# Decoder, last layer: expert weights loaded tile by tile and used as the stationary operand

## The chip, the cores and the metric

The kernel runs on one NeuronCore of a Trainium2 chip. The metric is the time of one execution on the device in microseconds. Each engine (TensorE for matrix products, VectorE or DVE, ScalarE or ACT, GpSimd or POOL, and SyncE or SP, which only issues transfers) runs its own program in order, and semaphores tie them together. A chance is later given for "faster", "same" and "slower"; 0.2% of the time is the bound between them.

## What is computed

The kernel is a decoder of two layers over 32 sequences of 128 tokens with 128 features. Only the last step of the second layer, a mixture of experts, is touched by the change:

```python
def _L1_ffn_ref(x, gate_W, W_gate, W_up, W_down):      # 8 experts, F = 512, top 2
    xf = x.reshape(B * T, D)                           # 4096 tokens x 128
    pi = _sinkhorn(-(xf @ gate_W.T))                   # 20 iterations
    _, top_idx = jax.lax.top_k(pi, TOP_K)
    g = jnp.einsum('nd,efd->enf', xf, W_gate)
    u = jnp.einsum('nd,efd->enf', xf, W_up)
    y = jnp.einsum('enf,edf->end', jax.nn.silu(g) * u, W_down)
    out = jnp.zeros_like(xf)
    for k in range(TOP_K):
        out = out + y[top_idx[:, k], n_ar] * pi[:, k:k + 1]
    return out
x = _layernorm(x + _L1_ffn_ref(x, ...), axis=-1)
```

## The kernel before

`sinkhorn_ffn` does this step. After the routing, the 8192 pairs of token and expert are sorted by expert into NT = 71 tiles of 128 rows, each tile belonging to one expert. `ids` holds for each tile the rows of the token table `XD` in DRAM, `te` the number of its expert. The program of the 71 tiles is written out, not a loop at run time.

A tile goes through these operations. GpSimd gathers 128 rows of `XD` by an indirect transfer into one of RB = 4 buffers `XG` (`gather`, L1629). TensorE transposes it (`x_transposed`, L1864), and DVE copies the result to `xT` (`x_copy`, L1776). TensorE multiplies with `xT` as the stationary operand and 512 columns of the expert's gate and up weights as the moving one (`gate_up`, L1871 and L1872); the weights of all experts, `wg` and `wu`, 2 MB each, lie in SBUF, loaded once by SyncE at the start of the stage, and the slice is picked by a register with the expert's number. ScalarE applies Silu to the gate (`gated`, L1675), DVE multiplies with up (`product`, L1783) into `H`, which has tokens on the partitions. TensorE transposes `H` in four blocks (`h_transposed`, L1879), ScalarE copies that to `HT` (`turned`, L1681), and TensorE makes Y in four products with the blocks of `HT` as stationary operands and the rows of `wd` as moving ones (`down`, L1887). DVE copies Y out (`y_copy`, L1789), and GpSimd scatters it to the table `YD` in DRAM (`scatter`, L1634).

The order of the work is fixed by hand on each engine. TensorE's turn i holds the transposition of tile i, gate and up of tile i-1, the transposition of H of tile i-2 and down of tile i-3. DVE's turn i holds the copy of xT of tile i, the product of tile i-1 and the copy of Y of tile i-3. GpSimd issues gathers 0 to 3 and then, for each i, gather i+4 and scatter i. Scatter i waits for the copy of Y of tile i (semaphore `yc`), and gather i+4 waits until `XG` is free (semaphore `xT`). TensorE reads the expert's number in each turn (`value_load`, L1893). Before the tiles, DVE works out `te` (L1765) and, after a product of TensorE, `ids` (L1770). After the tiles, SyncE waits for the last scatter, loads Y back in 16 pieces, and DVE adds the two experts' parts (`Acc`) and applies the normalization.

Each float32 product appears in the trace as two passes, each with its own load of the stationary side (a transposition as one).

Of the kernel before, what the change touches and what calls it, by code (L numbers as in the profile page):

```python
# [1527 lines left out]
def sinkhorn_ffn(c, W, wsem, wcount, out):  # L1528
# [6 lines left out]
    RB = 4  # L1535
# [4 lines left out]
    GATE, UP, HTB, XTB, YB = (0, 1), (2, 3), (4, 5), 6, 7  # L1540
# [3 lines left out]
                     "os ot rr id te wl we xT xTc gu sg h hT hTc y yc a2 x st mv lv rs2 out")  # L1544
    gs = list(c.sems("e_", " ".join(f"g{i}" for i in range(RB))).values())
    ys = list(c.sems("e_", " ".join(f"y{i}" for i in range(RB))).values())
    yl = list(c.sems("e_", " ".join(f"l{i}" for i in range(RB))).values())
    sl = {"st": s["st"], "mv": s["mv"], "lv": s["lv"], "rs": s["rs2"]}
# [25 lines left out]
    XG = sb("XG", [P, RB, D])  # L1574
    xT = sb("xT", [D, 2, P])
    Sg = sb("Sg", [P, 2, F])
    H = sb("H", [P, 2, F])
# [3 lines left out]
    Acc = sb("Acc", [P, 2, GB, D])  # L1581
# [12 lines left out]
    with nc.Block() as block:  # L1594

        @block.sync
        def _(sp):
# [3 lines left out]
            for n in late_weights():  # L1601
                full = tuple(slice(None) for _ in W[n].shape)
                sp.dma_start(W[n][full], c.dram[f"w6_{n}"]).then_inc(s["we" if n in ("wg", "wu", "wd") else "wl"], 16)
# [20 lines left out]
        def _(pool):  # L1624

            def gather(i):
                if i >= RB:
                    pool.wait_ge(s["xT"], i - RB + 1)
                nc.gpsimd.indirect_dma_start(out=XG[:, i % RB, :], out_offset=None, in_=XD[:, :],  # L1629
                                             in_offset=bass.IndirectOffsetOnAxis(ap=ids[:, i:i + 1], axis=0)).then_inc(gs[i % RB], 16)  # L1630
# [8 lines left out]
            for i in range(RB):  # L1639
                gather(i)  # L1640
            for i in range(NT):
                if i + RB < NT:
                    gather(i + RB)
                scatter(i)
# [4 lines left out]
        def _(act):  # L1649
# [27 lines left out]
            def turned(i):  # L1677
                act.wait_ge(s["hT"], i + 1)
                if i >= 2:
                    act.wait_ge(s["y"], i - 1)  # L1680
                nc.scalar.copy(HT[:, i % 2, :], bank(HTB[i % 2])).then_inc(s["hTc"], 1)  # L1681

            for i in range(1, NT + 2):
                if i - 1 < NT:
                    gated(i - 1)
                if 0 <= i - 2 < NT:
                    turned(i - 2)

        @block.vector
        def _(dve):  # L1690
# [81 lines left out]
            def x_copy(i):  # L1772
# [3 lines left out]
                nc.vector.tensor_copy(xT[:, i % 2, :], PS[:, XTB, 0:P]).then_inc(s["xTc"], 1)  # L1776

            def product(i):
                dve.wait_ge(s["gu"], 2 * i + 2)
                dve.wait_ge(s["sg"], i + 1)  # L1780
                if i >= 2:
                    dve.wait_ge(s["hT"], i - 1)
# [302 lines left out]
```

## Time and profile before

| | us |
|---|---|
| median of 3 runs | 2434.86 (2433.98 to 2436.57) |
| profiled execution, its own time | 2434.3 |
| its span in the trace | 2432.5 |
| mean granted clock of TensorE | 0.845 of full |

| engine | busy in the span |
|---|---|
| TensorE | 1741.1 us, 72% |
| DVE | 1712.0 us, 70% |
| ScalarE | 941.0 us, 39% |
| GpSimd | 803.8 us, 33% |

The times are those of one profiled execution. Engine names in the rows: PE is TensorE's product, PEld its load of a stationary operand, which runs beside products, PEldq and SPq the sequencers, POOL is GpSimd. In the timeline "xN" is the number of merged instructions, and what stands in brackets is the idle time ahead and what ended it. "issue" is time in which nothing shown was waited for. The stage of the tiles lasts from about 2081 us of the span to 2376, the tail from there to the end.

### The profile page before, as it was taken

How to read it: one execution, taken by the hardware profiler on the slowest of the kernel's cores; microseconds unless marked ns; L12 is line 12 of the kernel's file. 1: busy time of each engine (PE TensorE's matmuls, PEld its weight loads, DVE VectorE, ACT ScalarE, POOL GpSimd, SP SyncE). 2: the span in 40 equal slices, each digit the busy share in tenths (PEclk: the TensorE clock that was granted, in tenths of full speed). 3: DMA queues.
4: the chain of work that ended last, by engine and by line, in shares of the span. 5: the costliest groups of instructions: out<-in, count | busy, mean ns of one | idle time of the engine just before them, and what ended most of it. 6: DMA issues, size and time to landing. Idle time of an engine off the chain costs nothing. (4 is left out here: it accounts for less than half of the span.)

```text
span 2432.5 us, 29879 instructions
## 1 busy us (share of the span) xinstructions
PE 1741.1 (72%) x9233; PEld 1061.5 (44%) x9233; DVE 1712.0 (70%) x3432; ACT 941.0 (39%) x1424; POOL 803.8 (33%) x773
## 2 busy tenths in 40 slices
PE   6999965655589947777877877679997221788880
PEld 3555554654556612322322332256666110455550
DVE  4999966677668828888888889869995567333326
ACT  2444431122144446456446545345553221222230
POOL 2222211222110025666566556532220000344441
PEclk9999987777789968888878888989997555899995
DMA  4000000000000000000000000000002200011113
GB/s 119 1 0 0 1 11 6 0 5 0 0 1 0 0 9 1 1 1 1 0 0 0 0 0 1 0 9 6 5 3 76 106 1 0 24 33 33 33 31 107
DMA packets 38099, 38.05 MB, mean 16 GB/s; under 512 B 7261, under 2 KB 32965, under 8 KB 37493
## 3 DMA queue, kind: packets, MB, share of 16 engines
q1 hardware_dynamic: 33461, 27.60, 3.7%
q0 software_dynamic: 4544, 9.32, 1.3%
q8 instruction: 44, 0.72, 0.1%
q14 instruction: 50, 0.41, 0.1%
HBM read 25.69 MB, written 11.21 MB: 15 GB/s over the span
## 5 line engine op out<-in xcount | busy, mean ns | idle before, releaser
L1498 PE MATMUL PS<-m_hC,identf 128*128 128x512 f32 x512 | 331.9, 735 | 146.4 <-POOL m_hC L1256 140.8
L1256 POOL TENSOR_TENSOR m_hC<-m_h,m_Cs 128x512 f32<-128x512 f32 x256 | 337.6, 1327 | 227.5 <-DVE m_h L1391 150.4
L1391 DVE TENSOR_TENSOR_SCAN m_h<-m_dA,PS 128x512 f32<-128x512 f32 x256 | 312.4, 1220 | 30.4 <-ACT m_dA L1344 19.5
L1498 PEld LDWEIGHTS PS<-m_hC,identf 128*128 128x128 f32 x512 | 102.2, 224 | 289.8 <-POOL m_hC L1256 264.2
L1386 DVE TENSOR_TENSOR PS<-PS,m_DU 128x512 f32<-128x512 f32 x256 | 178.4, 697 | 31.7 <-PE PS L1471 19.1
L1344 ACT ACTIVATE m_dA<-m_DT,m_A 128x508 f32<-128x508 f32 x256 | 178.2, 716 | 25.2 <-DVE m_h L1391 23.9
L1349 ACT COPY m_Cs<-PS 128x512 f32<-128x512 f32 x128 | 74.4, 581 | 273.6 <-PE PS L1478 273.6
L1629 POOL DMA_INDIRECT e_XG<-token_rows,e_ids x71 | 69.2, 974 | 237.0 <-DVE e_ids L1770 215.7
L82 POOL TENSOR_TENSOR ln_lv<-ln_mv,ln_eps 128x4 f32<-128x4 f32 x40 | 8.1, 202 | 361.2 <-DVE ln_mv L75 361.2
L1783 DVE TENSOR_TENSOR e_H<-PS,e_Sg 128x512 f32<-128x512 f32 x71 | 49.1, 692 | 108.9 <-PE PS L1872 99.5
L1675 ACT ACTIVATE e_Sg<-PS 128x512 f32<-128x512 f32 x71 | 42.4, 598 | 195.9 <-PE PS L1871 189.5
L1634 POOL DMA_INDIRECT expert_rows<-e_Yo,e_ids x71 | 70.2, 988 | 132.9 <-DVE e_Yo L1789 130.4
L311 ACT COPY a_PT<-PS 128x1024 f32<-128x1024 f32 x63 | 63.8, 1012 | 88.3 <-PE PS L522 88.3
L278 ACT ACTIVATE a_E<-a_DD 128x1024 f32<-128x1024 f32 x64 | 67.7, 1058 | 54.9 <-DVE a_DD L380 53.7
L311 ACT COPY k_PT<-PS 77x1024 f32<-77x1024 f32 x63 | 63.5, 1008 | 61.8 <-PE PS L522 61.8
L378 DVE TENSOR_REDUCE a_mx<-PS 128x8 f32<-128x1024 f32 x64 | 77.3, 1208 | 7.7 <-PE PS L515 7.7
L384 DVE TENSOR_REDUCE a_sm<-a_E 128x8 f32<-128x1024 f32 x64 | 77.4, 1210 | 5.8 <-ACT a_E L278 5.8
L522 PE MATMUL PS<-identf,k_E 128*77 128x128 f32 x512 | 70.5, 281 | 15.1 <-ACT k_E L278 15.1
L380 DVE TENSOR_TENSOR a_DD<-PS,a_mx 128x1024 f32<-128x1024 f32 x64 | 78.4, 1224 | 2.2
L1871 PE MATMUL PS<-e_w_wg,e_xT 128*128 x142 | 79.3, 641 | 0.0
L1148 PEld LDWEIGHTS PS<-w_ew,f_G 128*128 128x128 f32 x512 | 64.7, 191 | 32.1 <-issue 25.9
L512 PE MATMUL PS<-k_BD,k_QM 128*128 128x308 f32 x256 | 78.3, 429 | 0.0
(347 smaller groups left out, 4110.7 us busy)
## 6 DMA issues: line engine op xcount, KB each, us to landing
token_rows<-X SPq DMA_DIRECT2D x2, 2048.0 KB, 12.2
e_Y<-expert_rows SPq DMA_DIRECT2D x16, 256.0 KB, 3.7
e_w_wg<-in_w_wg SPq DMA_DIRECT2D x1, 2048.0 KB, 8.0
e_w_wu<-in_w_wu SPq DMA_DIRECT2D x1, 2048.0 KB, 12.4
e_w_wd<-in_w_wd SPq DMA_DIRECT2D x1, 2048.0 KB, 16.9
out_dram<-X SPq DMA_DIRECT2D x8, 256.0 KB, 2.3
X<-in_x SPq DMA_DIRECT2D x1, 1792.0 KB, 7.5
x_Cs<-in_ctx SPq DMA_DIRECT2D x8, 154.0 KB
```

Of the source, the lines that this page charges most:

```text
L311: nc.scalar.copy(PT[:, u % 2], PS[0:KL, 4:6, :].rearrange("p i (h q) -> p (i h) q", q=P)).then_inc(s["pt"], 1)
L378: nc.vector.tensor_reduce(m, units(hf), AX_X, ALU.max).then_inc(s["mx"], 1)
L380: nc.vector.tensor_tensor(d, units(hf), mb, ALU.subtract).then_inc(s["d"], 1)
L384: nc.vector.tensor_reduce(sm[:, u * HU:(u + 1) * HU], E[:, u % 2], AX_X, ALU.add).then_inc(s["sm"], 1)
L512: ins = nc.tensor.matmul(scores(gp), q, BD[r, par, :, b, :], start=True, stop=cross)
L1256: nc.gpsimd.tensor_tensor(hC[:, i % ND, :], hst[:, i % ND, :], Cs[:, n % ND, :], ALU.mult).then_inc(s["hC"], 1)
L1344: nc.scalar.activation(dA[:, i % ND, :, 1:P], bl(DT[:, par, ch, :])[:, :, 1:P], ACT.Exp, scale=A[:, ch, n:n + 1]).then_inc(s["dA"], 1)
L1349: nc.scalar.copy(Cs[:, n % ND, :], bank(3)).then_inc(s["Cs"], 1)
L1386: nc.vector.tensor_tensor(bank(4), bank(1 + n % 2), DU[:, par, ch, :], ALU.mult).then_inc(s["dBu"], 1)
L1391: nc.vector.tensor_tensor_scan(hst[:, i % ND, :], dA[:, i % ND].rearrange("p b l -> p (b l)"), bank(4), 0.0, ALU.mult, ALU.add).then_inc(s ...
L1498: nc.tensor.matmul(bank(5 + ch), c.identf[:, :], hC[:, i % ND, :], start=(n == 0), stop=(n == NS - 1)).then_inc(s["yacc"], 1)
L1871: nc.tensor.matmul(bank(GATE[i % 2]), xT[:, i % 2, :], one(W["wg"][:, bass.ds(e, 1), :]), start=True, stop=True).then_inc(s["gu"], 1)
```

## The change

SyncE loads each tile's gate and up weights, 512 KB, from DRAM into one of RW = 6 buffers `WT`, by an address computed from the tile's expert. It reads the number itself (`value_load`), and from the seventh tile on it waits until gate and up of the tile six before are done. The 2 MB tensors `wg` and `wu` are no longer kept. The weights lie in DRAM so that a load is 128 rows of 4 KB.

TensorE uses blocks of 128 columns of `WT` as the stationary operand and `xT` as the moving one: eight products of 128 columns a tile in place of two of 512. Their results have the hidden features on the partitions, so DVE's product writes `HT` directly; the transposition of H, ScalarE's copy of it and the buffer `H` go. TensorE's turn i then holds the transposition of tile i, gate and up of i-1 and down of i-2.

The banks of PSUM that this frees make the results of the token transposition and of down double. The ring of gathered rows has RG = 8 buffers. GpSimd issues gathers 0 to 7 first and then gather i+8 and scatter i. DVE's turn starts with the copy of Y of tile i-3. `Acc` lies over `XL`, a buffer of the routing that is no longer in use. The names of the semaphores and the call that passes arrays are changed accordingly.

```diff
-    RB = 4
+    RB, RG, RW = 4, 8, 6
...
-    GATE, UP, HTB, XTB, YB = (0, 1), (2, 3), (4, 5), 6, 7
+    GATE, UP, XTB, YB = (0, 1), (2, 3), (4, 5), (6, 7)
...
-    XG = sb("XG", [P, RB, D])
+    XG = sb("XG", [P, RG, D])
...
-    H = sb("H", [P, 2, F])
...
-    Acc = sb("Acc", [P, 2, GB, D])
+    Acc = XL[:, :, :].rearrange("p i (b d) -> p i b d", b=GB)
+    WT = sb("WT", [D, RW, 2, F])
...
-                sp.dma_start(W[n][full], c.dram[f"w6_{n}"]).then_inc(s["we" if n in ("wg", "wu", "wd") else "wl"], 16)
+                sp.dma_start(W[n][full], c.dram[f"w6_{n}"]).then_inc(s["we" if n == "wd" else "wl"], 16)
+            sp.wait_ge(s["te"], 1)
+            for i in range(NT):
+                e = nc.sync.value_load(te[0:1, i:i + 1], min_val=0, max_val=NE - 1)
+                if i >= RW:
+                    sp.wait_ge(s["gu"], 2 * (i - RW) + 2)
+                sp.dma_start(WT[:, i % RW, :, :], c.dram["w6_wgu"][bass.ds(e, 1), :, :, :].rearrange("o d w f -> d (o w) f")).then_inc(wt[i % RW], 16)
...
             def gather(i):
-                if i >= RB:
-                    pool.wait_ge(s["xT"], i - RB + 1)
-                nc.gpsimd.indirect_dma_start(out=XG[:, i % RB, :], out_offset=None, in_=XD[:, :],
-                                             in_offset=bass.IndirectOffsetOnAxis(ap=ids[:, i:i + 1], axis=0)).then_inc(gs[i % RB], 16)
+                if i >= RG:
+                    pool.wait_ge(s["xT"], i - RG + 1)
+                nc.gpsimd.indirect_dma_start(out=XG[:, i % RG, :], out_offset=None, in_=XD[:, :],
+                                             in_offset=bass.IndirectOffsetOnAxis(ap=ids[:, i:i + 1], axis=0)).then_inc(gs[i % RG], 16)
...
-            for i in range(RB):
+            for i in range(RG):
                 gather(i)
             for i in range(NT):
-                if i + RB < NT:
-                    gather(i + RB)
+                if i + RG < NT:
+                    gather(i + RG)
                 scatter(i)
...
-            def turned(i):
-                act.wait_ge(s["hT"], i + 1)
-                if i >= 2:
-                    act.wait_ge(s["y"], i - 1)
-                nc.scalar.copy(HT[:, i % 2, :], bank(HTB[i % 2])).then_inc(s["hTc"], 1)
-
-            for i in range(1, NT + 2):
-                if i - 1 < NT:
-                    gated(i - 1)
-                if 0 <= i - 2 < NT:
-                    turned(i - 2)
+            for i in range(NT):
+                gated(i)
...
-                nc.vector.tensor_copy(xT[:, i % 2, :], PS[:, XTB, 0:P]).then_inc(s["xTc"], 1)
+                nc.vector.tensor_copy(xT[:, i % 2, :], PS[:, XTB[i % 2], 0:P]).then_inc(s["xTc"], 1)
...
-                    dve.wait_ge(s["hT"], i - 1)
-                nc.vector.tensor_tensor(H[:, i % 2, :], bank(UP[i % 2]), Sg[:, i % 2, :], ALU.mult).then_inc(s["h"], 1)
+                    dve.wait_ge(s["y"], i - 1)
+                nc.vector.tensor_tensor(HT[:, i % 2, :], bank(UP[i % 2]), Sg[:, i % 2, :], ALU.mult).then_inc(s["h"], 1)
...
             for i in range(NT + 3):
+                if 0 <= i - 3 < NT:
+                    y_copy(i - 3)
                 if i < NT:
                     x_copy(i)
                 if 0 <= i - 1 < NT:
                     product(i - 1)
-                if 0 <= i - 3 < NT:
-                    y_copy(i - 3)
...
-            pe.wait_ge(s["we"], 48)
+            pe.wait_ge(s["we"], 16)
 
             def x_transposed(i):
-                pe.wait_ge(gs[i % RB], landed(i))
-                if i:
-                    pe.wait_ge(s["xTc"], i)
-                nc.tensor.transpose(PS[:, XTB, 0:P], XG[:, i % RB, :], c.identf[:, :]).then_inc(s["xT"], 1)
-
-            def gate_up(i, e):
+                pe.wait_ge(gs[i % RG], 16 * (i // RG + 1))
+                if i >= 2:
+                    pe.wait_ge(s["xTc"], i - 1)
+                nc.tensor.transpose(PS[:, XTB[i % 2], 0:P], XG[:, i % RG, :], c.identf[:, :]).then_inc(s["xT"], 1)
+
+            def gate_up(i):
                 pe.wait_ge(s["xTc"], i + 1)
+                pe.wait_ge(wt[i % RW], 16 * (i // RW + 1))
                 if i >= 2:
                     pe.wait_ge(s["h"], i - 1)
-                one = lambda ap: ap.rearrange("p o f -> p (o f)")
-                nc.tensor.matmul(bank(GATE[i % 2]), xT[:, i % 2, :], one(W["wg"][:, bass.ds(e, 1), :]), start=True, stop=True).then_inc(s["gu"], 1)
-                nc.tensor.matmul(bank(UP[i % 2]), xT[:, i % 2, :], one(W["wu"][:, bass.ds(e, 1), :]), start=True, stop=True).then_inc(s["gu"], 1)
-
-            def h_transposed(i):
+                for w, banks in enumerate((GATE, UP)):
+                    for f in range(FC):
+                        ins = nc.tensor.matmul(PS[:, banks[i % 2], f * P:(f + 1) * P], WT[:, i % RW, w, f * P:(f + 1) * P], xT[:, i % 2, :], start=True, stop=True)
+                    ins.then_inc(s["gu"], 1)
+
+            def down(i, e):
                 pe.wait_ge(s["h"], i + 1)
                 if i >= 2:
-                    pe.wait_ge(s["hTc"], i - 1)
+                    pe.wait_ge(s["yc"], i - 1)
                 for f in range(FC):
-                    ins = nc.tensor.transpose(PS[:, HTB[i % 2], f * P:(f + 1) * P], H[:, i % 2, f * P:(f + 1) * P], c.identf[:, :])
-                ins.then_inc(s["hT"], 1)
-
-            def down(i, e):
-                pe.wait_ge(s["hTc"], i + 1)
-                if i:
-                    pe.wait_ge(s["yc"], i)
-                for f in range(FC):
-                    ins = nc.tensor.matmul(PS[:, YB, 0:D], HT[:, i % 2, f * P:(f + 1) * P], W["wd"][:, bass.ds(e * FC + f, 1), :].rearrange("p o d -> p (o d)"), start=(f == 0), stop=(f == FC - 1))
+                    ins = nc.tensor.matmul(PS[:, YB[i % 2], 0:D], HT[:, i % 2, f * P:(f + 1) * P], W["wd"][:, bass.ds(e * FC + f, 1), :].rearrange("p o d -> p (o d)"), start=(f == 0), stop=(f == FC - 1))
                 ins.then_inc(s["y"], 1)
 
             expert = {}
-            for i in range(NT + 3):
+            for i in range(NT + 2):
                 if i < NT:
                     expert[i] = nc.tensor.value_load(te[0:1, i:i + 1], min_val=0, max_val=NE - 1)
                     x_transposed(i)
                 if 0 <= i - 1 < NT:
-                    gate_up(i - 1, expert[i - 1])
+                    gate_up(i - 1)
                 if 0 <= i - 2 < NT:
-                    h_transposed(i - 2)
-                if 0 <= i - 3 < NT:
-                    down(i - 3, expert.pop(i - 3))
+                    down(i - 2, expert.pop(i - 2))
...
-            "wg": ([D, 8, 512], F32), "wu": ([D, 8, 512], F32), "wd": ([P, 32, D], F32)}
+            "wd": ([P, 32, D], F32)}
...
-    w["w6_wg"], w["w6_wu"] = (a["L1_ffn_W_" + n].transpose(2, 0, 1) for n in ("gate", "up"))
+    w["w6_wgu"] = np.stack([a["L1_ffn_W_" + n].transpose(0, 2, 1) for n in ("gate", "up")], 2)
```

## Rows read from the trace of the kernel before

**Rows 1.** Busy time by stretch, with clock, DMA share, GB/s: start, middle of the tiles
```profile
2084.00:2092.00 8.00, 6.80 (x11) 3.02 (x12) 1.47 (x4) 1.20 (x2) 2.84 (x3) 0.57 0.13 33
2125.00:2250.00 125.00, 105.92 (x526) 68.81 (x524) 38.63 (x93) 36.70 (x62) 60.45 (x62) 1.00 0.12 34
```

**Rows 2.** Groups by line, 2081 to 2376: busy, mean ns, idle before and releaser
```profile
L1864 PE MATMUL PS<-identf,e_XG 128*128 128x128 f32 x71 | 22.4, 315 | 48.0 <-DMA e_XG<-token_rows,e_ids 48.0
```

**Rows 3.** Chain of waits over two tiles: start us, us, what
```profile
2168.62 0.33 PE PS L1864
2168.95 1.00 PE PS L1871 x2
2169.95 0.86 PE PS L1872 x2
2170.81 0.44 PE PS L1879 x4
2171.24 0.91 PE PS L1887 x8
...
2172.18 0.30 DVE e_Yo L1789
...
2172.74 0.99 POOL expert_rows L1634
...
2174.04 2.69 DMA e_XG<-token_rows,e_ids
```

**Rows 4.** Timeline of TensorE, one turn without a hole: start us, us
```profile
2092.58 0.27 PE L1864 MATMUL PS<-identf,e_XG 128*128 128x128 f32 x1
2092.69 1.02 PE L1871 MATMUL PS<-e_w_wg,e_xT 128*128 x2
2093.55 1.02 PE L1872 MATMUL PS<-e_w_wu,e_xT 128*128 x2
2094.41 0.60 PE L1879 MATMUL PS<-identf,e_H 128*128 128x128 f32 x4
2094.85 1.06 PE L1887 MATMUL PS<-e_w_wd,e_HT 128*128 x8
2095.74 0.27 PE L1864 MATMUL PS<-identf,e_XG 128*128 128x128 f32 x1
```

**Rows 5.** Third stage, line L1148: durations min/median/max ns, and eight passes in the timeline
```profile
L1148 PEld LDWEIGHTS PS<-w_ew,f_G x512: 186/192/192, 692.9 to 854.3; 128*128 128x128 f32 x171
...
702.56 1.05 PE L1148 MATMUL PS<-w_ew,f_G 128*128 128x128 f32 x8
```

**Rows 6.** GpSimd's gathers: durations min/median/max ns, and the first one
```profile
L1629 POOL DMA_INDIRECT e_XG<-token_rows,e_ids x71: 943/972/1209, 2081.4 to 2360.8; - x71
...
2081.43 1.21 POOL L1629 DMA_INDIRECT e_XG<-token_rows,e_ids  x1 [215.69 <-DVE e_ids L1770]
```

**Rows 7.** Reads and transfers: durations ns; last two: KB each, us to landing
```profile
L1893 PEldq TENSOR_LOAD <-e_te x71: 296/301/483, 2080.6 to 2361.3; - x71
L1765 DVE CAST e_te<-e_tef x1: 197/197/197, 2074.3 to 2074.3; 128x71 int32<-128x71 f32 x1
L216 SPq DMA_DIRECT2D k_Cs<-in_ctx x7: 296/297/315, 1589.8 to 1771.0; - x7
...
e_w_wg<-in_w_wg SPq DMA_DIRECT2D x1, 2048.0 KB, 8.0
...
e_w_wd<-in_w_wd SPq DMA_DIRECT2D x1, 2048.0 KB, 16.9
```

**Rows 8.** Busy time by stretch as in rows 1: stage start, tail start
```profile
1870.00:1885.00 15.00, 15.00 (x75) 15.00 (x74) 1.15 (x6) 3.54 (x7) 0.00 (x0) 0.50 1.00 280
2376.00:2380.00 4.00, 0.00 (x0) 0.00 (x0) 0.00 (x0) 0.00 (x0) 0.00 (x0) 0.50 0.62 182
```

**Rows 9.** Timeline: the last token transposition and the last scatter
```profile
2363.51 0.27 PE L1864 MATMUL PS<-identf,e_XG 128*128 128x128 f32 x1
...
2374.00 0.97 POOL L1634 DMA_INDIRECT expert_rows<-e_Yo,e_ids  x1 [0.77 <-DVE e_Yo L1789]
```

More of the change, by code:

```diff
@@ L1543, in sinkhorn_ffn @@
     s = c.sems("e_", "xd xTp xL lg la rm rd re rs rl ra cm cT gm dg gM cd ce cs ct cl ca t w mb rk v tt "
-                     "os ot rr id te wl we xT xTc gu sg h hT hTc y yc a2 x st mv lv rs2 out")
-    gs = list(c.sems("e_", " ".join(f"g{i}" for i in range(RB))).values())
+                     "os ot rr id te wl we xT xTc gu sg h y yc a2 x st mv lv rs2 out")
+    gs = list(c.sems("e_", " ".join(f"g{i}" for i in range(RG))).values())
     ys = list(c.sems("e_", " ".join(f"y{i}" for i in range(RB))).values())
     yl = list(c.sems("e_", " ".join(f"l{i}" for i in range(RB))).values())
+    wt = list(c.sems("e_", " ".join(f"w{i}" for i in range(RW))).values())
     sl = {"st": s["st"], "mv": s["mv"], "lv": s["lv"], "rs": s["rs2"]}
@@ L1788, in y_copy @@
                     dve.wait_ge(ys[i % RB], landed(i - RB))
-                nc.vector.tensor_copy(Yo[:, i % RB, :], PS[:, YB, 0:D]).then_inc(s["yc"], 1)
+                nc.vector.tensor_copy(Yo[:, i % RB, :], PS[:, YB[i % 2], 0:D]).then_inc(s["yc"], 1)
             for i in range(NT + 3):
+                if 0 <= i - 3 < NT:
+                    y_copy(i - 3)
                 if i < NT:
@@ L2073 @@
     lay = layout(a)
-    need = ["x", "ctx", "identf", "identb"] + [f"w{ph}_{n}" for ph, ws in plan_weights().items() for n in ws] + ["w4_cwr"] + [f"w6_{n}" for n in late_weights()]
+    need = ["x", "ctx", "identf", "identb"] + [f"w{ph}_{n}" for ph, ws in plan_weights().items() for n in ws] + ["w4_cwr"] + [f"w6_{n}" for n in late_weights()] + ["w6_wgu"]
     nc = _bacc.Bacc("TRN2", target_bir_lowering=False, num_devices=1)
```

## Prediction, made before the changed kernel was run

> **What bounds the kernel now.** I read the page first, then the busy time by stretch, then the chain of waits inside one stretch, then the timeline of the same instructions. The reader should see four things in that order. The expert stage, where the change lies, keeps TensorE busy 85% of a middle stretch at a granted clock of 1.00, the upper level of 2.4 GHz, with DMA at 0.12 [rows 1]. So TensorE is not quite the limit. The grouped view names what it waits for: 48.0 us idle ahead of the token transposition L1864, all until the gather of e_XG has landed [rows 2]. The chain of waits over two tiles gives the loop: TensorE 0.33 + 1.00 + 0.86 + 0.44 + 0.91 us, the copy of Y 0.30, the scatter's issue on GpSimd 0.99, then the next gather, 2.69 from issue to landing, and three hand-overs (about 0.6): 2168.62 to 2176.73, 8.1 us for two tiles [rows 3]. The cause is in the code: GpSimd queues gather i+5 behind scatter i, and scatter i waits for Y of tile i, which TensorE makes in turn i+3. Transposition i+5 stands only two turns later, so of each pair one turn (3.2) hides nothing. From transposition 3 (2092.58) to transposition 70 (2363.51) are 67 tiles in 270.93 us, 4.04 each [rows 4, 9].
>
> **The floor of TensorE before.** Early on the gathers are ahead and a turn has no hole: transpositions at 2092.58 and 2095.74, 3.16 us [rows 4]. Its parts by starts: token transposition 0.11, gate 0.86, up 0.86, H transposition 0.44, down 0.89. The gate starts at 2092.69 and up at 2093.55, so 512 columns in two passes take 0.86. The eight passes of down, 128 columns each and each with its own stationary load, start 2094.85 and give way at 2095.74: 0.111 each. The third stage's passes with weights as the stationary side show the same, eight in 1.05 of which the last lasts 0.275: 0.78 / 7 = 0.111 [rows 5].
>
> **The change part by part.**
>
> Gate and up: out go 4 passes of 512 columns (1.72), in come 8 products of 128 columns, two passes each: 16 x 0.111 = 1.78. Plus 0.06 us a tile. The form is that of the down product and of rows 5. Bounds for a pass: 0.107 (what a pass of 512 columns costs per 128, 0.43 / 4) and 0.112. I take 0.111, since the rows are of the very form.
>
> Transposition of H and ScalarE's copy of it: minus 0.44 on TensorE. The copy is off TensorE's path in full stream and gives nothing there; it gives its time once, at the drain. DVE's product writes the same bytes to HT.
>
> New turn: 0.11 + 1.78 + 0.89 = 2.78 us, if nothing is late.
>
> Gather ring of eight: gather i+9 is now queued behind scatter i, and Y of tile i is made in turn i+2, so six turns (16.7 us) lie ahead of its use. It needs 0.3 (copy) + 0.3 + 0.99 + 0.3 + 2.7 = 4.6. The wait of rows 2 goes. What is late next is GpSimd itself: a gather 0.972 [rows 6], a scatter 0.99 and behind each a gap of 0.30 (the scatter ends at 2173.73, the gather starts at 2174.04 [rows 3]), 2.56 a tile, 0.22 under TensorE. The eight gathers at the start, from 2081.43 on [rows 6], end near 2091.8, before scatter 0 can be wanted, at about 2093.6.
>
> Weights by SyncE: 71 loads of 512 KB (128 rows of 4 KB), 37 MB, where 4 MB came once before. SyncE's work for one: reading the expert's number, priced by TensorE's own, 0.30, then a transfer at a computed address, also 0.30, as k_Cs has it [rows 7]; with as much again for registers, range checks and the wait it is 1.2 us of 2.78, an estimate, and it would have to double to matter. Nothing is queued behind it on SyncE but the tail's loads, and the last weights are issued about five turns before the end. The ring's wait is for gate_up i-6, so about five turns, 14 us, are left for the landing. Cost of one transfer: the loads of wg and wd, two apart, landed 8.9 us apart although issued within 1 us, so 2 MB take 4.45 and 512 KB 1.1 us of all engines; from below, at the 280 GB/s of the 512-byte rows of token_rows, 1.9 us [rows 7, 8]. With the gathers and scatters, 0.12 of 4.04 = 0.5, DMA is busy 1.6 to 2.4 us of 2.78. It holds, and 14 us cover a landing of 3 to 5. That cover gone (a turn's weights one turn late) costs a whole 2.78 once, not per tile. The first six start at 2074.5, when the expert numbers are cast [rows 7], and the first is wanted once the first gather, issued at 2081.43, has landed (after 2084) and is transposed. They overlap the first gather: 0 to 0.5 us, I take 0.
>
> The Trainium skill, DMA: Bandwidth & Descriptors, "Anatomy of one DMA", fits 2.0 us plus bytes by 436 GB/s: 3.2 us for one such load. Were loads made one at a time, the sum would be 30 us higher; the trace overlaps the fixed part of queued loads, as the 8.9 us above show.
>
> DVE a tile: two copies of 0.29 and the product 0.69, 1.27 of work; the product can start 0.2 after the up product (2.09 into the turn) and ends at 2.78, and down of that tile is wanted 1.9 into the next turn. The earlier place of y_copy, the doubled banks XTB and YB, Acc laid over XL, and ScalarE with Silu alone each have at least 1 us of room: nothing. The two reads of 4 MB taken from the stage's start run beside the routing, on which nobody waits: nothing.
>
> **The sum.** Turns 0 to 2 run mostly at the lower level of the clock (0.57 granted, against 1.00 right behind it [rows 1]); they stream as many columns after as before, so I leave their time. Only turn 2 ends with down (0.89) where it had H's transposition (0.44): transposition 3 is at 2093.03. Transposition 70 is at 2093.03 + 67 x 2.785 = 2279.6. From there two turns less a token transposition (5.5 to the start of the last down, which the last product releases), 1.05, the copy 0.33, and a scatter that has to wait for the one before it (0.5 in all): 7.5 us, where it was 10.5 from 2363.51 to 2374.00 [rows 9]. The last scatter is at 2287.1, 86.9 us earlier; the tail is the same. The profiled execution took 2434.3 (span 2432.5): 2347.4. The median of the three runs lies 0.6 higher, 2434.86: **2348 us**. Of the gain, 67 x 0.88 = 59 us are the wait for gathers and 67 x 0.375 = 25 are TensorE's work.
>
> **Rivals.**
>
> GpSimd becomes the bound. The traffic of DMA grows fivefold beside it. The one price above the median is the first gather's 1.209 [rows 6]. If both operations cost that, a tile is 2 x 1.51 = 3.02: plus 17 us, 2365. It decides from 1.09 an operation on. For it: 92% load, no slack for jitter. Against: a spread of 943 to 1209 with all but few at 972. Chance 0.15.
>
> The weights' transfers pace the tiles. At the 182 GB/s of the stretch in which the tail's loads start [rows 8], the 655 kB of a tile (524 of weights, 65.5 each gathered and scattered) take 3.6 us: plus 58, 2406. One at a time at 3.2, the page's fit above, 2377. Against: those stretches are short of queued work, and a ring of six is not. Chance 0.09, half for each.
>
> Stationary loads no longer hide. Before, four of a turn's 17 passes load weights ahead of 512 columns; afterwards all 25 have 128 columns. A load shows 0.192 busy [rows 5]. If passes went at that, a turn is 24 x 0.192 + 0.11 = 4.72, 0.68 above 4.04: plus 46, 2481, slower than before. It decides at (4.04 - 0.11) / 24 = 0.164 a pass. Against: runs of eight at 0.111, in two stages; longer runs no row shows. Chance 0.03. The Trainium skill, TensorE: Matmul & The Clock Gate, "The mechanism" in Part 3, says that a stationary load overlaps a running matmul only where the row groups differ, which is this rival's rule; the rows of down disagree with it. Other ways to be slower (a stall of instruction supply, a late ring throughout): 0.02.
>
> The change does not loosen the loop: the scatter's landing, for which y_copy waits four tiles later, or an order I misread keeps 4.04. Then within a few us of before, 2432. Chance 0.03.
>
> **How the numbers follow.** Forecast 0.68 (2339 to 2356: the lower end is 0.107 a pass, 24 x 0.004 x 71 = 7 us, with a little of the start; the upper 0.1 us a turn of jitter), GpSimd 0.15, transfers 0.09, no loosening 0.03, slower 0.05. The range 2339 to 2385 holds the forecast, GpSimd and the page's serial case, some 0.87 nominally, and 8 in 10 once I allow for causes not named. A measurement tells about 0.2%, 5 us, from no change. Faster 0.92, same 0.03, slower 0.05.
>
> **What would show it.** Right: token transpositions 2.78 us apart; the token transposition's idle until the gather near nothing; passes with the weights WT at 0.111; GpSimd idle 0.2 a tile until e_Yo; DMA share 0.5 to 0.8 in the stage; the first weights landed before the first transposed tokens are there; the last scatter at 2287. Wrong: a TensorE wait on WT (transfers), GpSimd idle near zero with longer operations (GpSimd), passes further apart (loads), or a granted clock under 1.00 after the start.

## The result, and the profile after

| | before | after |
|---|---|---|
| median of the runs, us | 2434.76 (2433.98 to 2436.57) | 2376.64 (2376.30 to 2377.49) |
| ratio | | 0.9761, 95% interval 0.9744 to 0.9778 |
| span of the profiled execution, us | 2432.5 | 2374.5 |
| mean granted clock | 0.844 | 0.842 |

The kernel is 58.1 us faster. The forecast was 2348, a gain of 87, so 29 us of it did not come, although the time lies in the range. The runs below say which part came, and the trace says where the other part is lost; what causes the loss they leave open.

The busy time by stretch of the changed kernel: us, then busy (x instructions) of PE, PEld, DVE, ACT and POOL, clock, DMA share, GB/s. The first row answers to the middle stretch of [rows 1]; the last is taken where the gathers and the loads of weights are over.

```profile
2100.00:2200.00 100.00, 92.37 (x793) 88.82 (x792) 35.95 (x94) 19.11 (x32) 61.05 (x63) 1.00 0.67 206
2302.00:2310.00 8.00, 8.00 (x75) 8.00 (x73) 3.54 (x9) 1.67 (x3) 2.85 (x3) 1.00 0.09 27
```

TensorE has holes again, 7.6 us in 100; DMA went from 0.12 to 0.67, inside the forecast 0.5 to 0.8, and the clock is at its upper level in both stretches. The groups by line from 2070 to 2325 answer to [rows 2]:

```profile
L1871 PE MATMUL PS<-e_xT,e_WT 128*128 128x128 f32 x1136 | 144.9, 281 | 11.2 <-DVE e_xT L1774 9.8 <-issue 1.3
L1641 POOL DMA_INDIRECT expert_rows<-e_Yo,e_ids x71 | 70.1, 988 | 75.2 <-DVE e_Yo L1787 64.4 <-issue 10.8
L1636 POOL DMA_INDIRECT e_XG<-token_rows,e_ids x71 | 69.0, 972 | 237.1 <-DVE e_ids L1768 215.7 <-issue 19.8 <-PE PS L1862 1.5
```

The 48.0 us until a gather are gone. What TensorE waits for instead is VectorE's copy of the transposed tokens, L1774. GpSimd's operations last what they did, 0.97 and 0.99, and GpSimd is idle 64.4 us, 0.9 a tile, until Y is copied: it does not set the pace, it is kept waiting. The waits of TensorE, its side of loads (PEld) above all, and of SyncE's queue from 2095 to 2300 (us in total, times, longest) say the same. The only other result that TensorE waits for is DVE's product, four times, and no wait for weights is among them:

```profile
PEld PS L1871 <- DVE e_xT L1774: 14.5, 20, 0.8
PEld PS L1879 <- issue: 5.5, 5, 2.0
PE PS L1879 <- DVE e_HT L1781: 4.5, 4, 1.8
SPq L1610 <- PE PS L1871: 125.4, 56, 5.8
```

Why is the copy late, with 0.28 us of work in a turn of 2.79? The timeline of one turn and the next, 2203.8 to 2208.4 (start, us, engine, line; in brackets the idle time before):

```profile
2203.87 1.06 PE L1879 MATMUL PS<-e_w_wd,e_HT 128*128 x8
...
2204.76 0.27 PE L1862 MATMUL PS<-identf,e_XG 128*128 128x128 f32 x1
...
2204.87 1.95 PE L1871 MATMUL PS<-e_xT,e_WT 128*128 128x128 f32 x16
2205.87 0.97 POOL L1636 DMA_INDIRECT e_XG<-token_rows,e_ids  x1 [0.30 <-issue]
...
2207.55 0.27 PE L1862 MATMUL PS<-identf,e_XG 128*128 128x128 f32 x1
2207.79 0.29 DVE L1787 COPY e_Yo<-PS 128x128 f32<-128x128 f32 x1 [2.99 <-PE PS L1879]
2207.91 0.60 ACT L1682 ACTIVATE e_Sg<-PS 128x512 f32<-128x512 f32 x1 [4.14 <-PE PS L1871]
2208.00 0.28 DVE L1774 COPY e_xT<-PS 128x128 f32<-128x128 f32 x1
2208.33 0.97 PEld L1871 LDWEIGHTS PS<-e_xT,e_WT 128*128 128x128 f32 x8 [0.75 <-DVE e_xT L1774]
```

Where two rows of a timeline have "..." between them, rows are left out. Down ends at 2203.87 + 1.06 = 2204.93, the token transposition at 2205.03, and the gate, the first eight of the sixteen passes, at 2204.87 + 7 x 0.111 + 0.28 = 2205.93. VectorE and ScalarE stand idle and wait for these three results, yet take them up at 2207.79 and 2207.91: 2.9 us late for Y, 2.0 for Silu, and the copy of xT, third in line, 3.0. Two engines that don't wait for each other wake together, so what is late is TensorE's signal and not a consumer. From this TensorE loses 0.75. I call this "late signals". In the turns of tiles 67 to 70, behind the last gather (its issue starts at 2295.53), each result is taken up within 0.04 to 0.14 us of its pass, and turns are 2.79.

The trace also records when each semaphore was raised, and that shows it directly. The increment that belongs to the down of 2204.93 stands at 2207.77, the transposition's at 2207.80, those of gate and up at 2207.89 and 2207.99, and those of the next down and transposition at 2208.08 and 2208.11: six in 0.34 us. The scatter's landing, for which a copy of Y waits too, is not what is late: all 28 copies of Y that came over 0.3 us late to an idle VectorE start within 0.06 us of an increment for Y. (Where the increment stands over 1.5 us behind its pass, the view names no pass and says "remote".)

One regularity shows when the signals come. Between 2095 and 2295 there are 28 bursts of four or more increments less than 0.15 us apart. At the start of each GpSimd is idle, and its last operation was a gather, which ended 0.87 to 1.24 us before. The seven other kernels with late signals below show the same (169 bursts, 0.74 to 1.54 us). That ties the release in time to GpSimd's gathers. It does not show that they are the cause: GpSimd also comes to stand idle because the copy of Y is late, and other runs below have the same gathers and no late signal.

Over tiles 8 to 60 a copy of xT starts 2.16 us after the end of its transposition on average, and up to 4.3. A late start of up to about 2.2 us costs TensorE nothing, since the gate product is that much later in its queue; what goes beyond that is a hole, mostly in every second turn: 2.79, then 3.57. Three turns are longer still (5.27, 5.94 and 5.45, 8.3 us over 2.79 together); there down also waits 1.0 to 1.8 us for DVE's product. A fourth, of 4.51, has another reason. Behind the hole of 2270 to 2275 the granted clock went to its lower level for 3.4 us, and the sixteen passes of gate and up took 3.64 us instead of 1.95:

```profile
2270.00:2275.00 5.00, 2.98 (x26) 2.70 (x24) 1.68 (x4) 1.19 (x2) 2.27 (x3) 1.00 0.22 60
2275.00:2280.00 5.00, 4.95 (x30) 4.79 (x29) 1.27 (x3) 0.60 (x1) 3.33 (x4) 0.66 0.70 235
```

### The profile page after: what moved, and what is told of

Its sections match the earlier page's. It is cut to its first block and busy times, and to the rows that moved or that the text cites. A ratio compares the mean times of both kernels' runs of the same rounds, so it can differ in the third digit from the quotient of the medians.

```text
span 2374.5 us, 31088 instructions
## 1 busy us (share of the span) xinstructions
PE 1706.1 (72%) x9801; PEld 1104.6 (47%) x9801; DVE 1704.7 (72%) x3432; ACT 899.1 (38%) x1353; POOL 803.6 (34%) x773
## 5 line engine op out<-in xcount | busy, mean ns | idle before, releaser
L1871 PE MATMUL PS<-e_xT,e_WT 128*128 128x128 f32 x1136 | 144.9, 281 | 11.2 <-DVE e_xT L1774 9.8
L1871 PEld LDWEIGHTS PS<-e_xT,e_WT 128*128 128x128 f32 x1136 | 135.7, 195 | 16.8 <-DVE e_xT L1774 14.5
L1781 DVE TENSOR_TENSOR e_HT<-PS,e_Sg 128x512 f32<-128x512 f32 x71 | 49.0, 691 | 73.2 <-PE PS L1871 55.0
L1641 POOL DMA_INDIRECT expert_rows<-e_Yo,e_ids x71 | 70.1, 988 | 75.2 <-DVE e_Yo L1787 64.4
L1148 PEld LDWEIGHTS PS<-w_ew,f_G 128*128 128x128 f32 x512 | 64.7, 191 | 32.1 <-issue 25.8
```

The costliest lines, as they stand in the source:

```text
L1871: ins = nc.tensor.matmul(PS[:, banks[i % 2], f * P:(f + 1) * P], WT[:, i % RW, w, f * P:(f + 1) * P], xT[:, i % 2, :], start=True, stop=True)
```

## Experiments

Twelve kernels ran in three batches, each batch on a chip of its own; I call them chip A (the first four), B (the next four) and C (the last four). That turned out to matter. In the fences of code "..." stands for lines of the edit that are not shown. The kernel before measured 2435.22, 2436.41 and 2434.78 on them; on which chip the two executions shown above ran is not known.

**a_ring8: the gather ring alone (A).** The kernel before with eight buffers for gathered tokens and Acc laid over XL, products in the old form.

```
-    RB = 4
+    RB, RG = 4, 8
...
-    XG = sb("XG", [P, RB, D])
+    XG = sb("XG", [P, RG, D])
...
-                if i >= RB:
-                    pool.wait_ge(s["xT"], i - RB + 1)
+                if i >= RG:
+                    pool.wait_ge(s["xT"], i - RG + 1)
...
```

> The kernel before with one part of the change alone: the ring of gathered rows has eight buffers instead of four (Acc laid over XL to make room); wg and wu stay resident, H is still transposed. Theory: the gather's wait is gone and a turn is the 3.16 us of TensorE's own work, 67 x 0.88 = 59 us less than before, about 2376 us, which is the time of the changed kernel. Rival: something else in the loop holds the old kernel at 4.04 us a turn, 2435 us; or it lies in between if TensorE's signals arrive late here too.

Measured: 2376.43, ratio 0.9759 (0.9743 to 0.9775). The stretch 2100 to 2200, columns as above:

```profile
2100.00:2200.00 100.00, 100.00 (x537) 67.84 (x536) 37.36 (x96) 37.25 (x63) 61.72 (x64) 1.00 0.15 43
```

Turns are 3.16, with no hole. The ring alone brings as much as the whole change: 0.9759 against 0.9761. Signals are on time here but for a few: three of the 52 copies of xT of tiles 8 to 59 start over 0.3 us late. Those of tiles 59, 61, 63 and 65 start 0.96 to 1.30 us late (the first of them is one of the three), so the old form is not free of late signals on this chip. So the 25 us for TensorE's shorter turn are what is missing.

**b_noload: no loads of weights behind the first six (A).** SyncE stops after the first six tiles; the others multiply by those, so the stream of 512 KB loads is gone.

```
-            for i in range(NT):
+            for i in range(RW):
                 e = nc.sync.value_load(te[0:1, i:i + 1], min_val=0, max_val=NE - 1)
...
-                pe.wait_ge(wt[i % RW], 16 * (i // RW + 1))
+                pe.wait_ge(wt[i % RW], 16)
```

> The changed kernel in which SyncE loads only the first six tiles' weights; all later tiles use what lies in the ring (so most tiles are multiplied with the wrong expert's weights, TensorE's work is the same). Theory: what holds back TensorE's signals in the changed kernel comes with SyncE's stream of loads (its waits, reads, issues or bytes), so turns are 2.79 us as in the last six tiles, about 2350 us. Rival: the hold-up comes from TensorE's dense stream of stationary loads itself, or from GpSimd's transfers; then it stays at 3.2 us a turn, 2376 us.

Measured: 2388.49, ratio 0.9807 (0.9791 to 0.9824); DMA share 0.14, and it is slower, not faster. (Its first gather starts at 2085.36 of the span, the changed kernel's at 2081.11, so some 4 us of the 12 more stand ahead of the tiles.)

```profile
2100.00:2200.00 100.00, 88.09 (x735) 84.28 (x734) 34.77 (x88) 16.46 (x29) 57.65 (x59) 1.00 0.14 39
```

Signals are late by up to 4.4 us, and 12 of 100 us are holes. SyncE's stream of transfers is not needed for them.

**c_small: the same loads with 64 KB from the seventh tile on (A).** The rest of a buffer keeps the weights of earlier tiles.

```
+                n = F if i < RW else 64
...
-                sp.dma_start(WT[:, i % RW, :, :], c.dram["w6_wgu"][bass.ds(e, 1), :, :, :].rearrange("o d w f -> d (o w) f")).then_inc(wt[i % RW], 16)
+                sp.dma_start(WT[:, i % RW, :, 0:n], c.dram["w6_wgu"][bass.ds(e, 1), :, :, 0:n].rearrange("o d w f -> d (o w) f")).then_inc(wt[i % RW], 16)
```

> The changed kernel with the same 71 loads, reads and waits of SyncE, but from the seventh tile on only 64 of 512 columns of gate and up are loaded (64 KB instead of 512 KB; the rest of the weights is left from earlier tiles). If the bytes and their DMA traffic hold up the signals: about 2350 us, 2.8 us a turn. If SyncE's waits, reads or issues do: unchanged, 2376 us.

Measured: 2378.98, ratio 0.9773 (0.9756 to 0.9789), signals late. The bytes are not needed for it either.

**e_waith: SyncE waits for VectorE's h, not for TensorE's gu (A).**

```
-                    sp.wait_ge(s["gu"], 2 * (i - RW) + 2)
+                    sp.wait_ge(s["h"], i - RW + 1)
```

> The changed kernel in which SyncE's wait for a free buffer is on DVE's product of the tile six before (semaphore h) and not on TensorE's own semaphore gu; everything else is the same. If TensorE's signals are late because SyncE waits on one of them: about 2350 us. If bytes, reads or issues are the cause: 2376 us within 0.3%.

Measured: 2379.23, ratio 0.9768 (0.9752 to 0.9784), signals late. That SyncE listens to TensorE is not the cause.

**g_nogather: gathers for the first eight tiles alone (B).** Later tiles multiply the rows that lie in the ring.

```
             for i in range(NT):
-                if i + RG < NT:
-                    gather(i + RG)
                 scatter(i)
...
-                pe.wait_ge(gs[i % RG], 16 * (i // RG + 1))
+                pe.wait_ge(gs[i % RG], 16)
```

> The changed kernel in which GpSimd gathers only the first eight tiles (later tiles multiply the rows that lie in the ring, so most of the result is of the wrong tokens); one operation of GpSimd a tile, the scatter, is left. Theory A: TensorE's signals are held while GpSimd issues its indirect transfers back to back, which it does at 2.57 us of 2.79 a tile. Then with half of them turns are 2.79 us: about 2350 us. Theory B: TensorE's own dense stream of stationary loads holds its signals, whatever GpSimd does: 3.2 us a turn or more, 2376 to 2390 us.

Measured: 2353.53, ratio 0.9662 (0.9646 to 0.9678), turns of 2.79, signals on time. Taken alone this says that the gathers hold the signals. The next three say that it can't be taken alone.

**h_up256: a_ring8 with half an up product from the third tile on (B).** The other half is left out. A turn of the old form as short as the new one.

```
-                nc.tensor.matmul(bank(UP[i % 2]), xT[:, i % 2, :], one(W["wu"][:, bass.ds(e, 1), :]), ...)
+                n = F if i < 2 else F // 2
+                nc.tensor.matmul(PS[:, UP[i % 2], 0:n], xT[:, i % 2, :], one(W["wu"][:, bass.ds(e, 1), 0:n]), ...)
```

> The kernel before with the ring of eight, and from the third tile on the up product has 256 columns instead of 512 (half of up is left from earlier tiles, so the result is wrong): a turn of TensorE is 3.16 - 0.43 = 2.73 us, with the old form of products (weights as the moving side). Theory A (GpSimd's back-to-back transfers set the pace at which signals are late): late signals and turns well above 2.73, 3.0 or more, so 2365 us or more. Theory B (the new form's 25 stationary loads a turn): signals on time, 2.73 us, about 2376 - 29 = 2347 us.

Measured: 2346.83, ratio 0.9634 (0.9617 to 0.9650), turns of 2.73, signals on time with all the gathers at full pace.

**v_ahead: one more turn for the copy of xT (B).** xT gets four buffers, and each turn multiplies gate and up for the tile before last, so a late copy would be covered.

```
-    xT = sb("xT", [D, 2, P])
+    xT = sb("xT", [D, 4, P])
...
-                if 0 <= i - 1 < NT:
-                    gate_up(i - 1)
                 if 0 <= i - 2 < NT:
-                    down(i - 2, expert.pop(i - 2))
+                    gate_up(i - 2)
+                if 0 <= i - 3 < NT:
+                    down(i - 3, expert.pop(i - 3))
```

VectorE's order is shifted by a turn in the same way.

> The changed kernel with TensorE's pipeline one turn deeper: transposition of tile i, gate and up of i-2, down of i-3 in turn i, four buffers xT, DVE's order shifted alike. If the late signals are a delay of up to 3 us and no limit on their number, a turn more of room hides them: 2.79 us a turn, about 2351 us. If GpSimd or the signals have a throughput below one tile in 2.79 us, nothing is won: 2376 us.

Measured: 2350.23 (2348.07 to 2352.00), ratio 0.9651 (0.9635 to 0.9667). It was to hide late signals; in the trace there are none to hide: all 275 recorded increments for xT, gate, up and Y between 2095 and 2290 stand within 0.02 us of the end of their pass.

```profile
2100.00:2200.00 100.00, 100.00 (x899) 100.00 (x898) 42.61 (x108) 21.09 (x37) 69.99 (x72) 1.00 0.75 235
```

TensorE is full with 899 passes, against 793 in the changed kernel; DMA moves 235 GB/s, and TensorE waits for none of it in this stretch. A load lands 3.6 us after its issue (median), and one is issued every 2.79 us, so loads overlap.

**k_pad: the first block of gate and of up multiplied twice (B).** A turn of the new form as long as the old one.

```
-                    for f in range(FC):
+                    for f in (0, *range(FC)):
```

> The changed kernel in which the first block of gate and of up is multiplied twice (same result): 4 passes more, a turn of TensorE of 2.79 + 0.45 = 3.23 us, with the new form of products and even denser loads per column than the ring-only kernel. Theory A (pace of tiles against GpSimd's 2.57 us): signals on time, 3.23 us a turn, about 2350 + 30 = 2380 us, only 4 us more than the changed kernel. Theory B (dense stationary loads): the holds stay, and the padding adds to 3.19: 2400 us or more.

Measured: 2384.05, ratio 0.9791 (0.9775 to 0.9807), turns of 3.23, signals on time.

At this point no kernel on B, of whichever form, had late signals, and all of the new form on A had. The last batch was made to find what starts them, and it tested the chip as well.

**x_stall: v_ahead with a stall in turn 24 (C).** Transposition 24 also waits for gather 29. Up to there TensorE's instructions are those of v_ahead.

```
+                if i == 24:
+                    pe.wait_ge(gs[(i + 5) % RG], 16 * ((i + 5) // RG + 1))
```

> The version with one more turn between the copy of the transposed tokens and the gate product, with one wait added: in turn 24 TensorE waits until gather 29 has landed, which by the order of GpSimd's queue is about 4.9 us (copy 0.3, scatter 1.3, gather 1.0, landing 2.1, hand-overs) after Y of tile 20. Theory A (once out of step the loop stays so in any such kernel): behind the stall the signals are late and the turns average 3.2; 2350 + 5 + 46 x 0.4 = 2373. Rival B (the room of a turn for the copy is what keeps signals on time): turns of 2.79 right behind the stall, time 2350 + 5 = 2355.

Measured: 2389.57, ratio 0.9813 (0.9798 to 0.9828). The same stretch, long before the stall, of v_ahead on B (first fence) and of x_stall on C (second):

```profile
2100.00:2150.00 50.00, 50.00 (x451) 50.00 (x450) 21.25 (x54) 10.54 (x19) 35.03 (x36) 1.00 0.74 235
```

```profile
2100.00:2150.00 50.00, 46.78 (x398) 45.05 (x397) 17.37 (x45) 8.25 (x14) 30.41 (x31) 1.00 0.64 201
```

The same order of the same instructions makes 451 passes in 50 us there and 398 here. Four rows of x_stall show why: down ends at 2133.26 and the next gate at 2133.20 + 0.78 + 0.28 = 2134.26, and both are taken up together, 1.8 and 0.9 us later:

```profile
2132.20 1.06 PE L1881 MATMUL PS<-e_w_wd,e_HT 128*128 x8
...
2133.20 1.95 PE L1873 MATMUL PS<-e_xT,e_WT 128*128 128x128 f32 x16
...
2135.04 0.29 DVE L1787 COPY e_Yo<-PS 128x128 f32<-128x128 f32 x1 [1.53 <-remote]
2135.16 0.60 ACT L1682 ACTIVATE e_Sg<-PS 128x512 f32<-128x512 f32 x1 [3.06 <-PE PS L1873]
```

Neither theory had this: signals are late before the stall (tile 4 is transposed at 2098.07, tile 23 at 2158.99, 3.21 a turn) and behind it alike. The extra turn of room does not keep them on time. The stall, two turns of 10.15 and 5.38, cost 10 us and not 5. TensorE waited 7.4 us, and the clock did the rest: it stood at its lower level from 2164.7 to 2174.9, so that the turn behind the wait took 2.6 us more than 2.79.

```profile
2165.00:2174.00 9.00, 4.85 (x23) 4.88 (x24) 0.98 (x2) 0.60 (x1) 1.96 (x2) 0.50 0.07 18
```

**z_padfirst: the doubling of k_pad in the first 24 tiles alone (C).**

```
-                    for f in range(FC):
+                    for f in ((0, *range(FC)) if i < 24 else range(FC)):
```

> The changed kernel with the first block of gate and of up multiplied twice in the first 24 tiles only (the same values into the same place, so nothing is left out). With the doubling in all 71 tiles the turns were 3.23 us, every signal on time, and the profiled span 2380.7. Theory A (TensorE's signals come late only once the loop has been thrown out of step, and the start of the stage does that): 24 clean turns of 3.23, then 47 clean ones of 2.79; span 2380.7 - 47 x 0.445 = 2360, time 2362. Rival B (the late signals come back by themselves whenever the changed kernel's turn is 2.79 with one turn's room for the copy of the transposed tokens): turns of 2.79 and 3.57 in alternation from about tile 25 on, mean 3.2 or so, time 2376 to 2382.

Measured: 2381.21, ratio 0.9782 (0.9766 to 0.9798). The first 24 tiles are again the same work as on B, k_pad first, z_padfirst second:

```profile
2100.00:2160.00 60.00, 60.00 (x540) 60.00 (x539) 21.88 (x57) 10.94 (x19) 36.07 (x37) 1.00 0.62 204
```

```profile
2100.00:2160.00 60.00, 59.82 (x510) 57.86 (x510) 20.39 (x54) 10.75 (x18) 33.50 (x35) 1.00 0.58 188
```

540 passes against 510 in 60 us; the turns are 3.24 up to tile 9 and then alternate between 3.3 and 3.6. So k_pad's clean turns were no property of the longer turn. Behind tile 24 come turns of 2.79 and 3.57, as in the changed kernel. The time is B's, but B took the first 24 turns for clean.

**u_order: VectorE copies xT ahead of Y (C).**

```
-                if 0 <= i - 3 < NT:
-                    y_copy(i - 3)
                 if i < NT:
                     x_copy(i)
+                if 0 <= i - 3 < NT:
+                    y_copy(i - 3)
```

> The changed kernel with the two copies of VectorE in the other order: the copy of the transposed tokens no longer stands behind the copy of Y, so it has about 0.3 us more room of 2.79, and no more. Theory A (the late signals are started by whatever makes TensorE wait for that copy, and the room that it has sets how often): alternating waits go or are smaller, turns of 2.8 to 3.05, time 2350 to 2368. Rival B (the order inside VectorE has no part in it, the signals are 1.5 to 3 us late whatever waits for them): 2373 to 2377.

Measured: 2382.40, ratio 0.9783 (0.9768 to 0.9798). The 0.3 us more room bring nothing; signals are late by up to 5 us, which 0.3 does not cover. The time is above both theories' numbers; rival B's direction holds.

**y_first: v_ahead with the third load of weights held back until the first gather has landed (C).**

```
+                if i == 2:
+                    sp.wait_ge(gs[0], 16)
```

> The version with one more turn of room, with SyncE holding back the third and the further loads of weights until the first gather has landed. Theory A (the first loads of weights, 3 MB issued within a few us, are what made the first gather land about 3 us later than before): the first token transposition at about 2084.3 instead of 2086.9, time 2347.5. Rival B (the first gather is late for another reason, or the held-back weights become what is late): 2350, or up to 2353.

Measured: 2378.57, ratio 0.9772 (0.9759 to 0.9785). The first token transposition of the changed kernel, of x_stall and of y_first:

```profile
2086.95 0.47 PE L1862 MATMUL PS<-identf,e_XG 128*128 128x128 f32 x1 [7.79 <-DMA e_XG<-token_rows,e_ids]
```

```profile
2089.12 0.47 PE L1864 MATMUL PS<-identf,e_XG 128*128 128x128 f32 x1 [8.13 <-DMA e_XG<-token_rows,e_ids]
```

```profile
2082.93 0.47 PE L1864 MATMUL PS<-identf,e_XG 128*128 128x128 f32 x1 [4.77 <-DMA e_XG<-token_rows,e_ids]
```

Between x_stall and y_first, on one chip, lie 6.2 us, but the stage itself also begins at different times. The first gathers of the three:

```profile
2081.11 1.21 POOL L1636 DMA_INDIRECT e_XG<-token_rows,e_ids  x1 [215.73 <-DVE e_ids L1768]
```

```profile
2082.94 1.21 POOL L1636 DMA_INDIRECT e_XG<-token_rows,e_ids  x1 [215.71 <-DVE e_ids L1768]
```

```profile
2080.11 1.21 POOL L1638 DMA_INDIRECT e_XG<-token_rows,e_ids  x1 [215.22 <-DVE e_ids L1770]
```

From the start of the first gather to the first transposition are 5.84, 6.18 and 2.82 us; in the kernel before, without these loads, 2.8. So holding the loads back brings 3.4 us on chip C, as theory A said. The time says nothing on it, because signals are late all through the tiles (mean turn 3.27), which neither forecast had allowed for.

**What they say together.** Mean turn over tiles 8 to 60, and how many of the 52 copies of xT start over 0.3 us late. "Turn of TensorE alone" is the turn when nothing is late:

| | chip | turn of TensorE alone | mean turn | late of 52 |
|---|---|---|---|---|
| the changed kernel | not known | 2.79 | 3.28 | 49 |
| a_ring8 | A | 3.16 | 3.16 | 3 |
| b_noload | A | 2.79 | 3.44 | 35 |
| c_small | A | 2.79 | 3.30 | 49 |
| e_waith | A | 2.79 | 3.28 | 45 |
| g_nogather | B | 2.79 | 2.79 | 1 |
| h_up256 | B | 2.73 | 2.73 | 1 |
| v_ahead | B | 2.79 | 2.79 | 1 |
| k_pad | B | 3.23 | 3.24 | 1 |
| x_stall | C | 2.79 | 3.44 (3.25 without the stall's 10 us) | 41 |
| z_padfirst | C | 3.23, then 2.79 | 3.31 | 40 |
| u_order | C | 2.79 | 3.36 | 43 |
| y_first | C | 2.79 | 3.27 | 43 |

A few of these turns are long because the clock fell, as at 2275 in the changed kernel. The first gather starts between 2080.1 and 2085.4 in these runs, so the turns say more than total times a few us apart.

Three things are shown. First, within chip A, late signals come with the new form and little with the old (one kernel), and they do not hang on SyncE's stream of transfers, their bytes or its wait. Second, work that is identical for 24 tiles has them on C and not on B, with the gate and up products one turn later (v_ahead, x_stall) as with doubled passes (k_pad, z_padfirst); all four or five executions of each kernel agree within 0.4%, so it is not chance from one execution to the next. The chip is what is known to differ between the batches; whether it is the chip itself or something else that changed with the batch was not tried. (Two builds differ a little beside the chip, by one wait or by the products of later tiles; that this should matter from the first turns on was not tried apart.) Third, therefore, nothing that B showed can be credited to an edit: not that gathers are needed (g_nogather), not that a short turn of the old form is safe (h_up256), not that v_ahead cures anything. Left open is what holds the signals back (the regular distance of the bursts from a gather's end is the best lead), whether the changed kernel itself would reach 2350 on chip B, and whether h_up256 would have them on A or C. The changed kernel and v_ahead were never run on one chip, so 2350.23 is the fastest time of a complete kernel here, and not shown to be a better kernel.

## Why the prediction was right in direction and 29 us short in size

**The wait for gathers: right.** Taken alone (a_ring8) the ring closes the holes of TensorE that this wait made and brings 58.8 us, where this term was forecast at 59. It is as much as the whole change brings.

**A turn of TensorE: right, where signals are on time.** Transposition, sixteen passes and down take 2.79, forecast 2.78, in tiles 67 to 70 of the changed kernel and in v_ahead from transposition 4 on, whose 2350.23 is near the 2348 of the sum. The end too: last token transposition to last scatter is 2308.33 to 2315.84, 7.5 as forecast.

```profile
2308.33 0.27 PE L1862 MATMUL PS<-identf,e_XG 128*128 128x128 f32 x1
```

```profile
2315.84 0.97 POOL L1641 DMA_INDIRECT expert_rows<-e_Yo,e_ids  x1 [0.30 <-issue]
```

**The step that failed** is "each have at least 1 us of room: nothing", said of the place of y_copy, XTB, YB, Acc and ScalarE; the copy of xT, for which TensorE then waited, has no term in the sum at all. The room was right by the durations; that a signal of TensorE reaches its reader at once was taken from a trace in which they all do. In the changed kernel from transposition 3 (2094.58) to 70 (2308.33) are 213.75 us, 3.19 a tile, where the sum had 186.6: 27.2 us, nearly all that is missing. Of these 1.7 are the turn at the lower clock, and the rest goes with late signals. In the sum's terms, the 25 us of "TensorE's work" came out at about zero. The upper end of the forecast's own part of the range, 2356, allowed for 0.1 us a turn; it was 0.4. That 2376.64 still lies between 2339 and 2385 is luck: the range reached that far for the sake of two rivals, and neither came true.

**The start: small miss.** "First weights at 2074.5 cost 0 (0 to 0.5)" was short. The first transposition stands at 2086.95, 5.84 us behind the start of the first gather at 2081.11, where the kernel before has 2.8, and transposition 3 at 2094.58 for 2093.03: 1.55 us. I had put the landing of the first weights against the first tokens, but not what six loads of 512 KB in the queues do to the gather behind them; y_first shows that, 3.4 us up to the first transposition.

**The rivals.** GpSimd as the bound: refuted, 0.97 and 0.99 an operation throughout and 64.4 us idle for Y. The weights' transfers: refuted, no wait for WT behind the start, and v_ahead takes a load every 2.79 us. Its serial case, 2377, falls on the outcome, but by accident. One at a time at the Trainium skill's fit (DMA: Bandwidth & Descriptors, "Anatomy of one DMA", a fit for transfers that GpSimd issues, applied here to SyncE's), 3.2 us, a load every 2.79 would not go, and the 3.6 us from issue to landing in v_ahead are longer than that distance too. The fixed part of queued loads overlaps, as the rows of two loads had suggested. Stationary loads that no longer hide: refuted by v_ahead, 899 passes in 100 us, each with its own load, 0.111 each. There the trace disagrees with the rule of the Trainium skill's TensorE: Matmul & The Clock Gate ("The mechanism" in Part 3) that a load overlaps a running matmul only between different row groups; the opening of the same section also allows it into a background buffer, which would fit the 0.111. A loop not loosened: refuted by a_ring8. Slower than before: no run.

**What the forecast said would show it wrong** named a wait for weights, a full GpSimd, slow passes and a low clock. The first three did not come. A granted clock under 1.00 did, once for 3.4 us and behind a hole of TensorE, and cost 1.7 us. The wait that made the difference, for a copy that has 2 us of room, was not on the list.

## What to carry to other kernels

Give a loop that waits for a remote event a deeper ring first and measure that by itself: here a ring of eight for one of four brought by itself as much as the whole change. Before two runs are compared by a time in the span, subtract where the stage begins in each: in y_first that start turned 3.4 us into 6.2. Room for a hand-over is the time until it is needed less the latency of the signal, and that latency must be read in the trace after, on engines that stand idle while their input is complete. Two of them waking together is the sign, and the recorded times of the increments prove it. And when experiments run on different chips, put the kernel that is to be explained into every batch: the second batch looked like four findings until the third ran the same turns elsewhere.

## What the runs showed of the hardware that I had not expected

Signals of TensorE reached VectorE and ScalarE up to 5 us after the pass that gives them (2.16 on average for xT in the changed kernel), in bursts, in kernels whose DMA share was 0.14 as well as 0.67. In the same instructions on another chip the increments stood within 0.02 us of the pass's end, and the copy of Y started 0.04 us after it. The bursts of four or more began 0.74 to 1.54 us after the end of a gather's operation on GpSimd, with GpSimd idle, 197 times in eight kernels. From about tile 67 on, a few us behind the last gather, they are on time on A and C too; since g_nogather ran on B only, that gathers are needed is not shown. Loads of 512 KB at addresses from a register, one issued every 2.79 us, and the gathers and scatters beside them move 235 GB/s together, each load landing 3.6 us after its issue (median, v_ahead). Six such loads issued ahead of a gather of 64 KB put off the token transposition behind it by 3.4 us (2.82 us after the start of the gather in y_first, 6.18 in x_stall). Behind a hole or a stall of TensorE of several us the granted clock went to its lower level, for 3.4 us at 2275 in the changed kernel and for 10.2 us in x_stall, and gate and up took 3.64 us there instead of 1.95.
